# A Mamba-2 and ternary-FFN layer on eight cores: FFN rounds of nine slices instead of eight, and single buffers for two activations

## What is computed

```python
def _quantize(w):                       # w1, w2: [5632, 2048], w3: [2048, 5632]
    gamma = jnp.mean(jnp.abs(w))
    return jnp.clip(jnp.round(w / (gamma + EPS)), -1.0, 1.0)
def _bitlinear(x, w):
    return jnp.matmul(x, _quantize(w).T)
def _L0_ffn_ref(x, w1, w2, w3):
    hidden = sigmoid(_bitlinear(x, w1)) * _bitlinear(x, w2)
    return _bitlinear(hidden, w3)
x = x + _L0_attn_ref(_layernorm(x), ...)  # inside: yg = y * silu(z), then RMS norm and W_out
x = x + _L0_ffn_ref(_layernorm(x), w1, w2, w3)
```

## Time and profile before

| | us |
|---|---|
| runs of the kernel before, median of 3 | 6304.32 |
| lowest and highest of them | 6006.94, 6372.62 |
| profiled execution, time | 6000.5 |
| profiled execution, span of its slowest core (7) | 5999.0 |
| spans of the other cores | 5971.4 to 5996.0 |
| FFN of segment 1, about | 1949 to 3273 |
| FFN of segment 2, about | 5038 to 5989 |

### The profile page before, as it was taken

One profiled execution on the slowest core, in us unless ns is written; L12 is line 12 of the kernel. 1 busy time (PEld: TensorE's weight loads), 2 busy tenths in 40 slices (PEclk: granted clock), 3 DMA queues, 4 the chain that ended last, 5 costly groups with the idle time before them and its releaser, 6 DMA issues.

```text
span 5999.0 us, 59574 instructions; the slowest of 8 cores (5971.4 to 5999.0 us)
## 1 busy us (share of the span) xinstructions
PE 4542.9 (76%) x21348; PEld 2255.2 (38%) x21348; DVE 2263.4 (38%) x2629; ACT 1476.3 (25%) x1787; POOL 552.2 (9%) x1090
## 2 busy tenths in 40 slices
PE   3876777777664787777785498777797675999997
PEld 1324555433221333333332144555543222444443
DVE  2555555411323333333332377566412223122112
ACT  1455333363001323323221112333221001000000
POOL 0001333200000000000000001333200000000000
PEclk8886555698776898898898698555598777999999
DMA  3894111295330635535435042000143321222222
GB/s 110 212 248 145 30 30 30 75 253 130 67 70 25 201 136 168 177 129 200 142 132 194 17 78 40 2 2 2 19 74 67 70 53 52 68 71 74 81 85 91
DMA packets 144885, 577.01 MB, mean 96 GB/s; under 512 B 36947, under 2 KB 39252, under 8 KB 106580
## 3 DMA queue, kind: packets, MB, share of 16 engines
q1 hardware_dynamic: 76468, 398.76, 20.5%
q0 software_dynamic: 68128, 174.44, 13.1%
HBM read 589.57 MB, written 85.98 MB: 113 GB/s over the span
## 4 chain that ended last, share of the span: by engine, by line
PE 57%; DMA 17%; DVE 15%; ACT 6%; issue 3%; POOL 1%; DVEq 0%; SPq 0%; ACTq 0%; POOLq 0%
PE p_ip L921 9%; PE p_ip L1051 8%; PE p_ip L1060 7%; PE p_ip L278 7%; PE p_ip L843 6%; PE p_w L1111 5%; PE p_ip L1111 5%; PE p_ip L734 4%; DMA aX_gslab<-w1T_t 3%; DVE aW_woslab L905 2%; DMA aW_w2slab<-w2T_t 2%; DMA aX_gslab<-w3T_t 2%; DMA aW_w2slab<-w3T_t 2%; DMA aW_eacsrow<-aW_eacs 2%; DMA aX_gslab<-w2T_t 2%
## 5 line engine op out<-in xcount | busy, mean ns | idle before, releaser
L1051 PE MATMUL p_ip<-aH_h,aW_q 128*128 128x512 bf16 x2816 | 705.6, 414 | 389.6 <-DVE aW_q L1031 335.5
L921 PE MATMUL p_ip<-aA_xy,aW_woslab 128*128 128x512 bf16 x2048 | 525.2, 424 | 249.8 <-DVE aW_woslab L905 249.8
L1060 PE MATMUL p_ip<-aH_h,aW_q 128*128 128x512 bf16 x2816 | 622.1, 379 | 0.0
L1051 PEld LDWEIGHTS p_ip<-aH_h,aW_q 128*128 128x128 bf16 x2816 | 292.0, 105 | 796.3 <-issue 522.7
L278 PE MATMUL p_ip<-aW_stageR,aW_stageL 2*128 2x128 f32 x2048 | 510.8, 427 | 45.8 <-DMA aW_eacsrow<-aW_eacs 45.5
L278 PEld LDWEIGHTS p_ip<-aW_stageR,aW_stageL 2*128 2x128 f32 x2048 | 470.8, 325 | 108.3 <-issue 92.7
L734 PE MATMUL p_ip<-aH_h,aW_wslab 128*128 128x512 bf16 x1536 | 366.0, 399 | 157.4 <-DMA aW_wslab<-winT_t 72.0
L921 PEld LDWEIGHTS p_ip<-aA_xy,aW_woslab 128*128 128x128 bf16 x2048 | 216.3, 107 | 558.3 <-issue 368.6
L1060 PEld LDWEIGHTS p_ip<-aH_h,aW_q 128*128 128x128 bf16 x2816 | 275.6, 98 | 332.2
L1111 PE MATMUL p_w<-aA_hid,aA_q3l 128*128 128x512 bf16 x1408 | 339.8, 383 | 38.5 <-DVE aA_q3l L1088 20.2
L843 PE MATMUL p_ip<-aH_h,aW_wslab 128*128 128x512 bf16 x1408 | 326.1, 392 | 50.3 <-ACT aW_sz L850 20.8
(11 more groups left out here) (182 smaller groups left out, 6500.3 us busy)
## 6 DMA issues: line engine op xcount, KB each, us to landing
aW_wslab<-winT_t POOLq DMA_DIRECT2D x92, 512.0 KB, 6.3
aX_gslab<-w1T_t SPq DMA_DIRECT2D x44, 1024.0 KB, 8.0
aX_gslab<-w2T_t SPq DMA_DIRECT2D x44, 1024.0 KB, 6.5
aX_gslab<-w3T_t SPq DMA_DIRECT2D x44, 1024.0 KB, 7.1
aW_w1slab<-w1T_t SPq DMA_DIRECT2D x44, 1024.0 KB, 9.6
aW_w2slab<-w2T_t SPq DMA_DIRECT2D x44, 1024.0 KB, 6.1
aW_w2slab<-w3T_t SPq DMA_DIRECT2D x44, 1024.0 KB, 6.1
aW_woslab<-woutT_t POOLq DMA_DIRECT2D x32, 1024.0 KB, 8.8
```

The lines of the kernel that those rows point to most:

```text
L921: ev_mm = P.add(T, lambda t, par=par, lh=lh, ec=ec, pb=pb: t.matmul(pb[lh][:, :], B["woslab"][par][:, 128 * ec:128 * ec + 128], B["xy"][:, ...
L1051: ex1 = P.add(T, lambda t, par=par, lh=lh, k=k: t.matmul(B["p_Y"][lh][:, :], B["q1"][par][:, 128 * k:128 * k + 128], B["h1"][:, k, 512 * l ...
L1060: ex2 = P.add(T, lambda t, par=par, lh=lh, k=k: t.matmul(B["p_diff"][lh][:, :], B["q2"][par][:, 128 * k:128 * k + 128], B["h1"][:, k, 512 ...
```

## The change

`FFN_R` becomes 9, so that the 44 slices are done in five rounds, four with nine slices and a last one with eight; `hid` and `q3l` grow by a slot. `sig2` and `sz2` are dropped: every sigmoid writes `sig` and waits for the product of the slice before it, and every Silu of the gate loop writes `sz` and waits for the product of the block before it. Both segments are changed in the same way.

```diff
-FFN_R = 8
+FFN_R = 9
...
-    B["sig2"] = arA.alloc("sig2", [128, SEGL])
...
-    B["sz2@m3"] = arW.alloc("sz3b", [128, SEGL])
...
-            szb = B["sz@m3"] if par2 == 0 else B["sz2@m3"]
-            evs2 = P.add(A, lambda a, pfull=pfull, szb=szb: a.activation(szb[:, :], pfull[:, :], AF.Silu),
-                         waits=[ev_mm, ev_ygs[ec - 2] if ec >= 2 else None])
+            evs2 = P.add(A, lambda a, pfull=pfull: a.activation(B["sz@m3"][:, :], pfull[:, :], AF.Silu),
+                         waits=[ev_mm, ev_yg_prev])
             slot_free[par2] = [evs2]
-            evyg = P.add(V, lambda v, ec=ec, szb=szb: v.tensor_tensor(B["xy"][:, ec, :], B["xy"][:, ec, :], szb[:, :], ALU.mult),
+            evyg = P.add(V, lambda v, ec=ec: v.tensor_tensor(B["xy"][:, ec, :], B["xy"][:, ec, :], B["sz@m3"][:, :], ALU.mult),
                          waits=[evs2] + (ev_ssd_done if ec < 2 else []))
...
-        sigf = [None, None]
+        sigf = None
...
-                sgb = B["sig"] if li % 2 == 0 else B["sig2"]
-                es2 = P.add(A, lambda a, sgb=sgb: a.activation(sgb[:, :], B["p_ip"][0][:, :], AF.Sigmoid, scale=0.5),
-                            waits=[ex1, sigf[li % 2]])
+                es2 = P.add(A, lambda a: a.activation(B["sig"][:, :], B["p_ip"][0][:, :], AF.Sigmoid, scale=0.5),
+                            waits=[ex1, sigf])
                 x1pf = {0: es2, 1: es2}
-                eh2 = P.add(V, lambda v, li=li, sgb=sgb: v.tensor_tensor(
-                    B["hid"][:, li, :], sgb[:, :], B["p_ip"][1][:, :], ALU.mult),
+                eh2 = P.add(V, lambda v, li=li: v.tensor_tensor(
+                    B["hid"][:, li, :], B["sig"][:, :], B["p_ip"][1][:, :], ALU.mult),
                     waits=[es2, ex2, hidf[li]] + (mam_bar if ri == 0 and li < 2 else []))
                 x2pf = {0: eh2, 1: eh2}
-                sigf[li % 2] = eh2
+                sigf = eh2
```

## The result

| | before | changed |
|---|---|---|
| median of 42 runs, us | 6090.62 | 5978.2 |
| lowest and highest run | 5998.65, 6465.77 | 5959.75, 6351.24 |
| like for like, ratio changed / before | 1 | 0.9938, 95% interval [0.9914, 0.9962] |

Some executions of either kernel run up to 8% longer with a lower granted clock on some cores; the medians above mix these with the others, and so the ratio is made from undisturbed runs alone and profiles are read on undisturbed cores. The ratio is the measurement: 0.62% faster, 23 to 52 us of 6005, in the middle 37. That is clear of noise and within 2%.

The account below looks back on a forecast made before the run. TensorE, busy 76% of the span, was taken as the bound, so its idle time counts; -23.2 - 22.1 - 1.9 + 2.4 = -44.8 us from the profiled 6000.5 gave 5955.7 us, range 5937 to 6330.

Parts of the forecast that it names:

- case (d): Whole kernel: grouping helps, but the measured median lies higher, as in the runs shown; 6260 us, chance 0.30.
- Last phase hides its output: Each segment's last w3 phase: groups of eight cover output transfers; 52.9 becomes 57.3 us, 52.6 becomes 58.1, with more matmuls.
- long transfer: Last w3 phase: an output transfer holding its staging buffer 5.19 us costs 1.0 us; one per segment assumed.
- the passages: FFN, between two slices across a w3 phase: 6.8 us each beyond matmuls in the first segment, one fewer per segment.
- Plain changes of slice: First segment's FFN, between slices without a w3 phase: one more, at 9.15 us.
- Second segment: Second segment's FFN: -23.2 us from the w3 phases and -1.9 from one passage fewer.
- Edits at no cost: Sigmoid and gate loop: one sig and one sz buffer change nothing, 0 us.
- (a): Last w3 phases: losing idle time lowers the clock there; two add 97 us, time 6053 us, chance 0.03.
- (b): Last w3 phases: output transfers stay the bound; two add 55.5 us, time 6011 us, chance 0.05.
- (c): First segment's plain slice changes eat the gain, with four long transfers per segment: -38 us, 5963 us; within the forecast's 0.62.
- the rule of the Trainium skill on the peak-current limiter: Last w3 phases: dense matmuls on three cores hold the clock at 13/16; gain about 19 us instead of 44.8.

Follow-up runs that it names:

- a1: Kernel before with rounds of nine only, sig and sz keeping two buffers each: FFN of segment 1 1314.9 us, of segment 2 926.9.
- a3: Kernel before with the round of four slices done first instead of last: FFN of segment 1 1312.4 us, of segment 2 933.7.
- a4: Kernel before with four output staging buffers instead of two: FFN of segment 1 1312.1 us, of segment 2 933.8.
- c1: Changed kernel, first segment's next w1 load also waiting for the w3 load of the slice before: FFN of segment 1 1342.0 us.
- b5: Changed kernel with five rounds of 8, 8, 8, 10 and 10 slices: 0.9929 of before, FFN of segment 1 1306.9 us.
- c0: Changed kernel run once more, without edits, for a second profile: 0.9933 of before, FFN of segment 1 1315.8 us.
- a2: Kernel before with one sig and one sz buffer, rounds still of eight: FFN of segment 1 1327.0 us, of segment 2 950.3.

## Why the prediction was right or wrong

**The number was wrong as a forecast of the time.** I put 5955.7 us, made from the profiled 6000.5, beside a median of 6304.32. Read against that median it says -5.5%, and no such gain exists: the measured medians are 6090.62 and 5978.2, like for like -0.62%. The step that failed is the last one of the sum, taking the level of one profiled execution as the level of the time. I had named the other level as case (d), with 0.30, and widened the range for it, which holds 5978.2; but a difference of 44.8 us can't be told from such a level, and the forecast should have been stated and judged as a ratio. As a ratio it is 0.9925, within the measured interval. That 5978.2 lies only 22 us from 5955.7 is luck: the median of before moved from 6304.32 to 6090.62 without any change to that kernel. Two ends of the range were added up wrongly, without effect on it: half of 27.6 is 13.8 and not 15, and the likeliest case reaches up to 5977 and not 5985.

**Last phase hides its output: right.** 57.3 and 58.1 us were forecast with one long transfer each; core 3 has 58.4 in the second segment, the mean of eight cores 60.0 in the first. DVE's waits for the output DMA did nearly vanish, with TensorE idle for 4.5 us behind DVE instead of under 3 + 3. a1, a3 and a4 show it from both sides. What I read wrongly inside it: I gave the whole 25 us to the transfer. a4 gives back 16; some 5 are DVE's eviction with two banks, which a3 shows with no transfer in sight. The sum did not suffer, as eight matmuls cover both.

**The mis-sized term: the passages.** I took 6.8 us as the price of a passage and let one of five go. The four that are left cost 33.6 us, as much as the five before (33.9), so the term was -0.3 and not -6.8. The price was a mean over passages that all stood behind an eighth slice, and it is not a constant: the ninth slice falls more often on the long side of an alternation that stands in the idle times before each slice, and that the order of DVE's work makes (see behind c1). I averaged that alternation away as 9.15. b5 shows that the term comes back, 5.6 us, with even rounds and the same number of passages. I had put a passage's bounds at 5.6 to 9.6, but applied them to the passage that goes and not to those that stay.

**Plain changes of slice:** one more for 9.15 forecast; +12.5 (c0) and +12.3 (a1) measured, 9.2 each. Right within the scatter of the cores (their sums spread over 15 us). With the 6.5 us of the passages these 3 us make up nearly all of what the first segment won less than forecast (9.2 us for 19.7).

**Second segment:** -25.1 forecast, -23.7 measured (-24.4 against the same four cores before); the 1.0 us by which core 7's last phase before (52.9) lay above the mean of the cores (51.9) explains most of it.

**Edits at no cost: right.** a2 shows no effect of one `sig` and one `sz`; the gate loop and the sigmoid did not move.

**Rivals.** (a) The granted clock in the last phase of core 3 is 1.00, as in the dense stretch before it; it did not fall. (b) The output transfers are not the bound. (c) was the nearest in kind, since the passages ate 6.5 us, though not by the way it named. By the rule of the Trainium skill on the peak-current limiter (TensorE: Matmul & The Clock Gate, Part 1: The HAM clock gate) the gain would have been 19 us, as an estimate; it is 33 by stages and 37 by the ratio, and cores 0 to 3 show 1.00. The 13/16 of that rule does appear in the same profile: on cores 6 and 7 the last phase of the second segment takes 68.3 and 68.9 us, and core 7's granted clock in it is 0.81 (6044 to 6110 us). What starts and ends it isn't shown by any run here.

## What to carry to other kernels

The last part of a blocked loop often has another limit than the rest: here a remainder of four made groups too short to cover eviction and output transfer, and spreading the remainder (or putting it first, or two more staging buffers) won 9 to 24 us per segment with not one matmul fewer. Before pricing "one wait fewer" by a mean, print the waits by their place in the round: if they alternate, moving the boundary by one changes what the remaining ones cost. And where a wait alternates, look for a short operation that stands in order behind a long wait and sets a shared buffer free, as the w3 sum does behind the hid product. And let the first groups behind a late operand run all but that operand's part.

## What was not expected of the hardware

With two PSUM banks a group of matmuls can be too short: at 0.216 us a matmul, 0.34 us until DVE starts, 0.69 for its eviction and 0.15 until TensorE is back, groups of four come 1.02 us apart and not 0.86 (a3), with DVE busy two thirds of the time. By the same sum, an estimate, groups of five would still be 0.05 us late each and groups of six not at all; groups of eight are not late (0.216 us a matmul). The 256 KB output transfers, 2.1 us from issue to landing, went through at 161 GB/s per core with two buffers and at 237 GB/s with four (a4), with the same time to landing. Of two loads of 1 MB issued 0.4 us apart the first took 6.2 us, against 6.1 without the other beside it, and the second 9.7 instead of 5.7 (c0 and c1, core 5). And in a loop that repeats exactly TensorE's wait went 5.8, 9.2, 7.6, 6.3, 8.5, 5.7, 8.9 us in the mean of eight cores: that is no property of the loads, whose own time differed by 1 us, but of the order of the work and of the buffer that w2 and w3 share.
